# The first cross layer's division: reciprocals by logarithm and exponential on ScalarE with a Newton step on VectorE

## The reference, cut to what matters

```python
def step(carry, kv_t):
    p, q, o = carry
    kt, vt = kv_t
    no = jnp.maximum(o, u + kt)
    A = jnp.exp(o - no)
    E = jnp.exp(u + kt - no)
    y = (A * p + E * vt) / (A * q + E)
    no2 = jnp.maximum(w + o, kt)
    A2 = jnp.exp(w + o - no2)
    E2 = jnp.exp(kt - no2)
    return ((A2 * p + E2 * vt, A2 * q + E2, no2), y)
...
x = x + _L0_xattn_ref(8, 128, 256, w, u, _layernorm(x), ctx_2048)
x = x + _L0_ffn_ref(_layernorm(x), router_w, gate_w, up_w, down_w)
```

## Time and profile before

| | us |
|---|---|
| median of 3 runs | 1528.91 (1528.41 to 1533.25) |
| profiled execution | 1531.77 |
| its span | 1530.0 |
| TensorE busy | 1384.1 (90%) |
| VectorE busy | 912.6 (60%) |
| ScalarE busy | 766.3 (50%) |
| GpSimd busy | 456.7 (30%) |

### The profile page before, as it was taken

The page is one execution under the profiler, slowest core; times in us unless marked ns, Lnnn a source line. Parts: engine busy times, 40 slices in busy tenths (PEclk is TensorE's granted clock), DMA queues, the critical chain, the costliest instruction groups (busy, mean ns, idle before and its releaser), DMA issues.

```text
span 1530.0 us, 25564 instructions
## 1 busy us (share of the span) xinstructions
PE 1384.1 (90%) x9742; PEld 865.6 (57%) x9760; DVE 912.6 (60%) x1665; ACT 766.3 (50%) x1847; POOL 456.7 (30%) x400
## 2 busy tenths in 40 slices
PE   7869999999899879999999998898997789889799
PEld 3434556555466545666667773665664545545536
DVE  7784322224578654555556688854787587676631
ACT  3452111111777566777776446457776545363230
POOL 3230000000000168786882000120742435314200
PEclk9979999999999999999999999998998898987989
DMA  8020221001200300000000100020001100000000
GB/s 256 28 83 1 67 59 34 1 0 73 92 2 2 125 0 8 7 8 8 8 7 1 76 23 1 1 83 1 2 2 72 56 0 3 3 1 3 30 0 28
DMA packets 21854, 48.12 MB, mean 31 GB/s; under 512 B 1506, under 2 KB 16995, under 8 KB 20580
## 3 DMA queue, kind: packets, MB, share of 16 engines
q1 hardware_dynamic: 21732, 46.47, 8.7%
HBM read 41.22 MB, written 5.24 MB: 30 GB/s over the span
## 4 chain that ended last, share of the span: by engine, by line
PE 68%; DVE 18%; ACT 6%; issue 4%; POOL 4%; DMA 0%; DVEq 0%; ACTq 0%; POOLq 0%
PE PS L862 49%; PE PS L1094 5%; DVE work L2568 5%; PE PS L1153 3%; PE PS L959 3%; PE PS L863 3%; ACT work L1697 2%; PE PS L876 2%; PE PS L1191 2%; DVE small L2040 1%; DVE work L2186 1%; DVE X L2547 1%; DVE work L2536 1%; POOL work L795 1%; PE PS L864 0%
## 5 line engine op out<-in xcount | busy, mean ns | idle before, releaser
L862 PE MATMUL PS<-XT,WB 128*128 128x512 f32 (+1 forms) x688 | 300.5, 595 | 5.1 <-DVE XT L2066 2.8
L862 PEld LDWEIGHTS PS<-XT,WB 128*128 128x128 f32 (+1 forms) x688 | 127.1, 191 | 149.7 <-issue 145.8
L1697 ACT ACTIVATE work<-PS,small 128x128 f32<-128x128 f32 x512 | 137.2, 415 | 45.9 <-DVE small L2371 45.8
L2261 DVE TENSOR_TENSOR work<-PS,work 128x512 f32<-128x512 f32 x48 | 33.1, 691 | 170.1 <-PE PS L862 170.1
L1625 ACT ACTIVATE work<-PS 128x512 f32<-128x512 f32 x48 | 28.7, 597 | 194.6 <-PE PS L862 194.6
L647 POOL TENSOR_SCALAR small<-small 128x4 f32<-128x4 f32 x22 | 5.0, 229 | 402.2 <-DVE small L2043 402.1
L2371 DVE TENSOR_REDUCE small<-PS 128x4 f32<-128x512 f32 x128 | 80.4, 684 | 41.4 <-PE PS L862 40.1
L862 PE MATMUL PS<-XT,WA 128*128 128x512 f32 (+2 forms) x224 | 98.4, 615 | 4.8 <-DVEq L2571 2.5
L2568 DVE SCALAR_TENSOR_TENSOR work<-PS,vec,work 128x508 f32<-128x508 f32 (+2 forms) x108 | 80.2, 742 | 14.3 <-DVE work L2568 7.2
L1094 PE MATMUL PS<-WB,work 128*128 128x256 f32 x384 | 86.9, 379 | 0.5 <-DVE work L2266 0.5
L1094 PEld LDWEIGHTS PS<-WB,work 128*128 128x128 f32 x384 | 72.8, 190 | 18.3 <-issue 7.7
(11 more groups left out here) (377 smaller groups left out, 2860.2 us busy)
## 6 DMA issues: line engine op xcount, KB each, us to landing
WB<-in_l0f SPq DMA_DIRECT2D x8, 768.0 KB, 7.6
WB<-in_l1x SPq DMA_DIRECT2D x1, 6144.0 KB, 19.2
WB<-in_l0f SPq DMA_DIRECT2D x32, 96.0 KB, 6.8
WB<-in_l2f SPq DMA_DIRECT2D x1, 3072.0 KB, 10.2
WA<-in_l3a SPq DMA_DIRECT2D x1, 2624.0 KB, 8.9
WB<-in_l3f SPq DMA_DIRECT2D x1, 2064.0 KB, 7.6
WA<-in_l1f SPq DMA_DIRECT2D x1, 2056.0 KB, 10.0
C<-in_ctx SPq DMA_DIRECT2D x2, 1024.0 KB, 7.0
```

The lines of the kernel that those rows point to most:

```text
L862: mm = lambda o, l, r, s, e: nc.tensor.matmul(o, l, r, start=s, stop=e)
L1697: f(wk(12288 + (u % 8) * G + h * P, P), bank(j)[:, h * P:(h + 1) * P], ACT.Exp, bias=sm(704 + (u % 8) * 4 + h, 1)).then_inc(*act_step(*([j ...
L2261: v.tensor_tensor(l0f_h(m)[:, lo:lo + G], bank(j), l0f_s(m)[:, lo:lo + G], ALU.mult).then_inc(*dve_step(j))
```

## The change

VectorE no longer calls the reciprocal in this layer. It goes through both halves up to the numerators and denominators, and adds to a new semaphore, `sums_final`, when the denominators of a half are done. ScalarE, in its loop over the blocks, ahead of block 4 (first half) and block 5 (second half), waits for it, writes the logarithm of e over ek and the exponential of its negative over that, r = exp(-ln e). A second loop of VectorE waits for each half's r and makes a Newton step: kp = e x r, ek = (kp - 2) x r, y = ev x (-1) x ek; then it overwrites the first positions as before.

```diff
@@ ScalarE, loop over the blocks
             for b in range(NB + 2):
+                if b in (4, 5):
+                    _, ek, _, e = l0x_tiles(b - 4)
+                    act.wait_ge(sums_final, b - 3)
+                    f(ek, e, ACT.Ln).then_inc(*act_step())
+                    act.wait_ge(*act_last())
+                    f(ek, ek, ACT.Exp, scale=-1.0).then_inc(*act_step(act_to_dve))
                 if b < NB:
@@ VectorE, first cross layer
                 v.scalar_tensor_tensor(b3(e)[:, :, 1:P], b3(qs_)[:, :, 0:P - 1], later, b3(e)[:, :, 1:P], ALU.mult, ALU.add).then_inc(*dve_step())
                 dve.wait_ge(*dve_last())
+                dve.sem_inc(sums_final, 1)
                 v.scalar_tensor_tensor(b3(ev)[:, :, 1:P], b3(ps_)[:, :, 0:P - 1], later, b3(ev)[:, :, 1:P], ALU.mult, ALU.add).then_inc(*dve_step())
-                v.reciprocal(e, e).then_inc(*dve_step())
-                dve.wait_ge(*dve_last())
-                v.tensor_tensor(y, ev, e, ALU.mult).then_inc(*dve_step())
+            for c in range(2):
+                ctxv, y = xt(c, 0, N, CT), wk(c * N, N)
+                kp, ek, ev, e = l0x_tiles(c)
+                dve.wait_ge(act_to_dve.sem, act_to_dve.next())
+                v.tensor_tensor(kp, e, ek, ALU.mult).then_inc(*dve_step())
+                dve.wait_ge(*dve_last())
+                v.scalar_tensor_tensor(ek, kp, 2.0, ek, ALU.subtract, ALU.mult).then_inc(*dve_step())
+                dve.wait_ge(*dve_last())
+                v.scalar_tensor_tensor(y, ev, -1.0, ek, ALU.mult, ALU.mult).then_inc(*dve_step())
                 dve.wait_ge(*dve_last())
                 v.tensor_copy(b3(y)[:, :, 0:1], b3(ctxv)[:, :, 0:1]).then_inc(*dve_step(*([dve_to_pe] if c else [])))
```

More of the change, by code:

```diff
@@ L287, in build @@
         ident_in, vec_in, pick_ready = sem("ident_in"), sem("vec_in"), sem("pick_ready")
-        windows_zero = sem("windows_zero")
+        windows_zero, sums_final = sem("windows_zero"), sem("sums_final")
         expert_b, eb_in = WB[:, 8192:8192 + 8 * D], sem("eb_in")
```

## The result

| | before | after |
|---|---|---|
| median, 9 runs each | 1528.65 | 1537.21 |
| profiled execution (span) | 1531.77 (1530.0) | 1537.39 (1535.6) |
| VectorE busy | 912.6 | 906.0 |
| ScalarE busy | 766.3 | 776.1 |

The ratio is 1.0053, with a 95% interval of 1.0037 to 1.0068: the changed kernel is slower by 8.1 us (5.7 to 10.4). The forecast was 6.9 us slower, a median of 1535.8 in a range of 1531.0 to 1539.0.

The account below looks back on a forecast made before the run. VectorE's chain to y bounds the kernel, ScalarE's ordered block work only 1.87 us ahead. Two pairs add 8.9 us there, so y's transposes start 6.9 later: 1538.7 profiled, median 1535.8, range 1531.0 to 1539.0.

Parts of the forecast that it names:

- VectorE before the reciprocals: VectorE's first loop in the cross layer: half 1 follows half 0 at once and ends at 82.84 us.
- VectorE after them: VectorE's second loop: three operations replace reciprocal and product, 4.04 us a half instead of 7.94, saving 7.8.
- The pairs: ScalarE's Ln and Exp of one half with their loads, ahead of blocks 4 and 5: 4.45 us each, two 8.9.
- Number of loads: ScalarE's table loads for two Ln and two Exp: four, one set per function, 1.31 us each.
- the one-load rival: On ScalarE one table serves Ln and Exp: 5.5 us of work, plus 3.5, 1532.4; one or no load 0.25.
- What waits: TensorE's last kt waits for ScalarE's scaled keys, moving 8.9 us; y's transposes behind it start 6.9 later.
- the lead: TensorE's 1.87 us between last kt and y's transposes: all that ScalarE's block work is ahead of VectorE.
- The clock: TensorE's idle times may lower its clock, at most 1.9 us more; taken as nothing, chance of loss 0.13.
- 5.3 us of room for eight products: TensorE's last pair of blocks: time for eight products, up to 7.2 us at low clock, before ScalarE needs them.
- The rival that the clock rises: The kt before y keeps TensorE at 2.4 GHz to the router, saving 2.2 us; not slower, chance 0.04.
- The second hole: TensorE's idle time between blocks, a block after the first one: 4.3 us again.
- The total: Whole kernel: plus 6.9 us on the profiled 1531.77, 1538.7; put on the median, 1535.8.

Follow-up runs that it names:

- e4_one_load: The changed kernel with a second Ln where Exp stood, so y is not the quotient; ratio 1.0011 against before.
- e2: The changed kernel without ScalarE's Ln and Exp and without the waits for them, reciprocals left out; ratio 0.998 against before.
- e10_half_y_early: The changed kernel with half 1 by VectorE's reciprocal again and y's transposes ahead of the last two kt; ratio 0.997 against before.
- e3_grouped: The changed kernel with Ln, Ln, Exp, Exp together ahead of block 5; ratio 1.0027 against before.
- e12: Changed kernel, but only half 0 by Ln (block 4), Exp (block 5) and Newton, half 1's reciprocal first, y's transposes early; ratio 0.9963 against before.
- e1: The kernel before with ScalarE's Ln and Exp added ahead of blocks 4 and 5, results unread, VectorE unchanged; ratio 1.0041 against before.
- e5: The changed kernel with the four transposes of y ahead of the last two kt; ratio 1.001 against before.
- e11: The changed kernel with half 1 by VectorE's reciprocal again, y's transposes still behind the last kt; ratio 1.0024 against before.
- e6: The changed kernel with Ln, Ln, Exp, Exp ahead of block 5 and y's transposes ahead of the last two kt; ratio 1.0011 against before.

## Why the prediction was right

- **VectorE before the reciprocals**: half 1 ended its last sum at 82.42, 22.87 us behind kp; predicted 82.84, 22.64 behind. The raising of `sums_final` adds a gap of about 0.1 ahead of L2192 in each half.
- **VectorE after them**: 3.95 us a half (82.99 to 86.94), predicted 4.04. scalar_tensor_tensor takes 1.23 at 1024 columns, the lower bound's neighbour. y came 2.64 us earlier, predicted 2.7.
- **The pairs**: Ln 1.06 (1.05 predicted), four loads of 1.28. kt to kt a pair adds 4.5 (77.47 to 85.88 is 8.41 for a block with a pair, 85.88 to 94.35 is 8.47; a block of the kernel before takes 3.87 to 3.93); 4.45 predicted.
- **Number of loads**, the choice on which the sum hung: four. Ln behind Exp and Exp behind Ln each load in the trace of after. The rule of the Trainium skill, "ScalarE: Activation LUTs", Table sets: the hidden batching unit, that one load serves ln and exp, is not what these traces show; the one-load rival was priced at +3.5 and e4_one_load, which has one load in the stage as the rule promises, measured +3.17.
- **What waits**: the last kt moved by 9.18 us (44.86 behind kp; 35.68 before), predicted 8.9, and y's transposes by 7.10, predicted 6.9. The difference between the two, 2.08, is the lead: the 1.87 of idle time and the 0.2 seen in e2, which the prediction had in its 0.95 from kt to transposes (0.88 measured). VectorE, not kt, was late before. e2_no_pairs shows the lead itself, 2.04.
- **The clock**, costed at nothing: a hole of 4.37 us came where 4.3 was predicted, and granted clock fell to 0.57:

```profile
86.00:90.00 4.00, 4.00 (x9) 1.95 (x9) 0.91 (x2) 3.87 (x4) 0.34 (x1) 0.57 0.19 71
90.00:94.00 4.00, 1.64 (x4) 0.38 (x2) 2.47 (x3) 3.87 (x15) 1.38 (x2) 1.00 0.04 14
```

  (Windows of the changed kernel: stretch, length, busy us of PE, PEld, DVE, ACT, POOL, PEclk, DMA, GB/s.) In the single us from 86 to 90 the granted clock was 0.64, 0.50, 0.50 and 0.66, so it was back after about 3 us, as the prediction had read it from 44 to 48 us of before. The eight products took 5.24, 1.64 more. ScalarE was in its second pair then, and its waits in this stretch are the usual 0.18.
  The prediction's reason for nothing, that the clock's return within 3 us leaves no loss, doesn't hold in general, and its 5.3 us of room for eight products are too many: ScalarE's next squares also wait for the kt behind those products. In e10_half_y_early products of 4.69 us already made ScalarE wait 1.17, in e3_grouped products of 5.09 made it wait 1.56. So costing the clock at nothing gave the right number here by luck: the second pair, by standing where it does, gave TensorE the time to catch up. The prediction did not say so.
- **The rival that the clock rises**: it didn't. The last kt, directly before y's transposes, took 1.09 as before, the granted clock from 104 to 106 was 0.50, and from y's transposes to the router it takes 15.34 us (15.36 before).
- **The second hole** was 2.71 us, not 4.3 again: the slow products filled a part of it.
- **The total**: the stage gives 7.1 of the 8.1 us. The remaining 1.0 lies within the interval, and nothing here tells whether it is real. The two profiled executions differ by 5.6 us, less than their stages do, so outside the stage the changed kernel's was 1.5 us shorter.

## What to carry to other kernels

Before moving work off the engine that ends last, find the lead of the engine that takes it: here 1.87 us (2.04 in effect), against 8.9 of new work, of which more than half was table loads. If the receiving engine works in order, the place in its order counts as much as the length; moving the urgent transposes ahead of work for a later layer was worth 6.9 us, and nothing until ScalarE was the one that ended last. Where an engine feeds TensorE, try cutting extra work for it into short pieces: here the same 4.5 us cost TensorE's clock in one piece and not in two.

## What the runs showed of the hardware

- A VectorE reciprocal takes 6.55 us on 128x1024, 5.3 times a product of the same shape (1.23). The three operations of the Newton step take 3.68 together.
- A table load costs 1.31 us from the end of one operation to the start of the next between an Ln and an Exp (changed kernel, 80.59 to 81.90), even where a wait stands between, and 1.39 behind an eviction (78.14 to 79.53): it begins 0.02 to 0.10 us after the operation. An Exp behind Ln loads as an Ln behind Exp does.
- TensorE's clock after a hole: behind holes of 2.0 (e12) and 3.09 us (e4_one_load) the next kt took 0.63 and eight products 3.60, all at 2.4 GHz. Behind 4.35 to 4.38 us (changed, e1, e5, e10, e11) eight products took 4.59 to 5.29, and behind 6.29 and 6.30 us (e6, e3) 4.96 and 5.09. In between it went either way: before, a kt behind 3.30 us idle took 0.63, and in e2_no_pairs one behind 3.31 us took 1.09, though TensorE's rows ahead of the two are alike. These runs don't settle the border.
